# Another order of the pieces of five interleaved sequences on four engines

## What is computed

```python
def _L0_attn(x):            # block A and C of the kernel
    q, k, v = split(x @ W_qkv.T + b_qkv)               # 8 heads of 16
    qq, kq, vq = encode(q), encode(k), encode(v)        # x / |x| * exp(i * phase)
    q_ent, k_ent = entangle(qq), entangle(kq)           # 3 layers of gates between neighbouring heads
    pattern = einsum('bsid,bsjd->bsij', conj(q_ent), k_ent)   # heads against heads, in each row
    for c in range(4):                                  # 4 circuits
        probs = softmax(g[c] * abs(pattern) ** 2)
        weighted = einsum('bsij,bsjd->bsid', sqrt(probs + 1e-12), vq) * coh
        final += sup_w[c] * clipped(weighted)
    return real(final) @ W_out.T + b_out
def _L0_ffn(x):             # block B: silu(x @ wg.T) * (x @ wu.T) @ wd.T, hidden 384
def _L1_attn(x):            # block E and part of D: causal attention, 16 heads of 8, 256 rows
def _L1_ffn(x):             # part of D (routing) and the stage behind the loop: 8 experts,
                            # each takes its 64 best rows of a sequence, gelu, 512 hidden
```

## Time and profile before

| | us |
|---|---|
| median of 3 runs | 2605.27 |
| lowest and highest of them | 2596.32, 2612.04 |
| the profiled execution | 2586.84 |
| its span, first to last instruction | 2585.0 |
| DVE busy | 1998.8 (77%) |
| PE busy | 1995.3 (77%) |
| POOL busy | 1428.3 (55%) |
| ACT busy | 1283.5 (50%) |
| granted clock of PE, mean | 0.882 |

### The profile page before, as it was taken

How to read it: one execution, slowest core, us unless ns; L and a number is a source line. 1 busy time by engine, 2 the same in 40 slices (tenths; PEclk the granted TensorE clock), 3 DMA queues, 4 the chain that set the end, 5 groups by cost and what they waited for, 6 DMA issues and landing times.

```text
span 2585.0 us, 45044 instructions
## 1 busy us (share of the span) xinstructions
PE 1995.3 (77%) x15068; PEld 1548.3 (60%) x15068; DVE 1998.8 (77%) x3422; ACT 1283.5 (50%) x2989; POOL 1428.3 (55%) x1104
## 2 busy tenths in 40 slices
PE   1357877888877888787788788888788787289999
PEld 0346666666666666666666666666666664157777
DVE  4888999989989998999999999899999852502221
ACT  1125555555555555555555555555555555033332
POOL 2666666666666665666666666666666510364310
PEclk8688899889899988989988988888988887589999
DMA  3000000000000000000000000000000000112210
GB/s 89 2 7 9 9 8 8 8 8 8 8 8 8 9 9 6 8 9 9 8 8 8 8 8 8 8 8 8 8 8 6 6 5 5 34 44 63 56 45 24
DMA packets 64565, 39.38 MB, mean 15 GB/s; under 512 B 9350, under 2 KB 60431, under 8 KB 64528
## 3 DMA queue, kind: packets, MB, share of 16 engines
q1 hardware_dynamic: 54238, 26.30, 3.6%
q0 software_dynamic: 4096, 8.40, 1.2%
q10 hardware_dynamic: 6194, 4.21, 0.6%
HBM read 26.31 MB, written 12.58 MB: 15 GB/s over the span
## 4 chain that ended last, share of the span: by engine, by line
POOL 32%; PE 25%; issue 19%; DVE 17%; ACT 5%; ACTq 1%; POOLq 0%; DVEq 0%; DMA 0%
POOL arena L649 10%; POOL arena L657 8%; PE pa L1296 4%; PE pd L1286 4%; DVE arena L629 4%; PE pb L1036 4%; POOL arena L461 4%; POOL arena L662 3%; POOL arena L629 3%; POOL arena L458 2%; PE pa L732 2%; DVE arena L525 2%; PE pd L1027 2%; DVE state L529 2%; PE pd L1024 2%
## 5 line engine op out<-in xcount | busy, mean ns | idle before, releaser
L751 PE MATMUL pa<-ident,arena 128*128 128x128 f32 x4096 | 545.9, 291 | 99.9 <-POOL arena L629 66.4
L751 PEld LDWEIGHTS pa<-ident,arena 128*128 128x128 f32 x4096 | 514.8, 205 | 122.7 <-POOL arena L629 79.9
L649 POOL TENSOR_TENSOR arena<-arena,neg_half 128x32 f32<-128x32 f32 x64 | 269.4, 4226 | 281.9 <-DVE arena L495 281.9
L1036 PE MATMUL pb<-ident,arena 128*128 128x128 f32 x1536 | 304.7, 313 | 138.2 <-ACT arena L931 84.2
L657 POOL TENSOR_TENSOR arena<-state,c_cross 128x448 f32<-128x448 f32 x128 | 241.6, 1908 | 226.6 <-DVE state L518 188.2
L1036 PEld LDWEIGHTS pb<-ident,arena 128*128 128x128 f32 x1536 | 194.6, 158 | 271.4 <-issue 172.9
L931 ACT ACTIVATE arena<-pb 128x384 f32<-128x384 f32 x512 | 253.9, 496 | 155.9 <-PE pb L1036 151.3
L629 DVE TENSOR_TENSOR arena<-arena 128x1024 f32<-128x1024 f32 x192 | 311.8, 1638 | 4.1 <-PE pa L751 3.3
L924 ACT ACTIVATE arena<-pd,arena 128x256 f32<-128x256 f32 x512 | 245.7, 480 | 0.0
L458 POOL TENSOR_TENSOR arena<-arena,eps_t 128x2 f32<-128x2 f32 x128 | 126.8, 991 | 213.4 <-DVE arena L490 125.8
L923 ACT ACTIVATE arena<-pd,arena 128x128 f32<-128x128 f32 x512 | 189.6, 370 | 37.7 <-DVE arena L811 36.6
(11 more groups left out here) (246 smaller groups left out, 4577.0 us busy)
## 6 DMA issues: line engine op xcount, KB each, us to landing
x_land<-in_L_attn_query SPq DMA_DIRECT2D x32, 128.0 KB, 2.1
arena<-in_L_attn_query SPq DMA_DIRECT2D x32, 128.0 KB, 2.1
x_scratch<-x SPq DMA_DIRECT2D x32, 128.0 KB, 1.8
xn_scratch<-xn_d SPq DMA_DIRECT2D x32, 128.0 KB, 1.8
arena<-x_scratch SPq DMA_DIRECT2D x16, 256.0 KB, 3.0
out_x<-arena SPq DMA_DIRECT2D x16, 256.0 KB, 2.4
w<-in_L_ffn_W ACTq DMA_DIRECT2D x1, 2048.0 KB
arena<-xn_scratch,arena POOLq DMA_INDIRECT x128, 2.5
```

What stands on the lines that cost most here:

```text
L649: g.tensor_tensor(of_tile(rnorm)[:, :, c], of_tile(ssq)[:, :, c], of_tile(neg_half)[:, :, c], ALU.pow).then_inc(S("a_rnorm"), 1)
L751: mm = pe.matmul(pa[:, t, c * P:c * P + P], wprod[:, k % NWP, j * 128:j * 128 + 128], ident[:, :], start=(j == 0), stop=(j == NH - 1))
L1036: mm = pe.transpose(pb[:, j * P:j * P + P], p_raw[:, s % 3, j * P:j * P + P], ident[:, :])
```

## The change

Only the four order strings change. The pieces, their number and the waits in them stay as they are.

```diff
-POOL_ORDER = "A1C2B1A3C1A1B1A2C1D1C1D1"
-ACT_ORDER = "E7A1E3A1E4B1E2A1E5B1E1C1E1B1E2C1E3A1E2B1E3C1E4A1E3C1A1D1B1D1C1D2"
-PE_ORDER = "E5A1E3A1E4B1E3B1E7B1E2B1E3C1E1C1E1C1E1C1D1C1D1C1D1C2D2C2"
-DVE_ORDER = "C1A1C1A1C1B1C1E1C1E1B1C1E1C2E1C1A1C1A1C1E1C4B1C1B1E1C2A1E1B1C1B1C1A1E1A1B1C1A1C2B1A1B1C1A2C1A1D2C1A1C1D3C1A2C2D2A1D1A1D1C1"
+POOL_ORDER = "A1C2B1A4C1B1A2C1D1C1D1"
+ACT_ORDER = "E7A1E1A1E3A1E5B1E4B1E3C1A1E2B1E3C1E3B1A1E2C1E6A1E1B1D1C1D1C1D2"
+PE_ORDER = "E4A1E1A1E6B1E4B1E7B1E2B1E3C1E1C1E1C1E1C1D1C1D1C1D1C2D2C2"
+DVE_ORDER = "C1A1C1A1C1B1C1E1B1E1C2A1E1C1A1C1E1C2E1C2A1C1E1A1C1B1C1B1A1C1E1A1C2B1C1B1C1E1B1A1C1A1C2B2A2C2A1D2C2D3C1A2C2D2A1D2A1C1"
```

## The result

The changed kernel takes 2469.24 us (median of 4, 2466.69 to 2473.79) against 2606.97 for the kernel before; the ratio is 0.948, interval 0.945 to 0.951. The profiled span fell from 2585.0 to 2464.9, by 120.1.

A forecast was written before the change was run, and what follows sets the result against it. Bound: DVE and POOL taking turns on two-operand SBUF work, the lap ended by a chain beginning on POOL. 28 laps x (64.2 - 61.9) = 64 us; 2586.8 - 64 = 2523, median 18.4 above: 2541, range 2512 to 2605.

The forecast's parts named there:

- the layout: New lap laid out by hand from old durations, each wait at its latest releaser: lap 61.9 us, 64.2 before.
- PE at offsets 5 to 17: Early qkv at 1.2 GHz: L494 and E3 each wait 0.9 us; DVE 0.2 behind at E4, bounds 0 to 2.
- rival 3: Slower: PE at 1.2 GHz past offset 15.9 delays scores of pairs 3 and 4, and k=0, by 1.4 us; chance 0.13.
- turns at 1.2 GHz past offset 16: Sign on PE that would show the prediction wrong.
- The unrolled laps: Laps outside the loop: same pieces with less to collide, nothing taken for them, bounds -6 and +6 us.
- Powers: POOL's L649 pair runs from 15.2 to 23.6 and does not block DVE; nothing charged.
- rival 2: No gain: waits at E3 and blocking return it; lap 64.2, chance 0.12. Strict form: powers hold L564 2.2 us, lap 64.1.
- Blocking: Two-operand work of DVE and POOL never runs together; losses 5.9 us a lap before, 3.6 blocked in the new lap.
- The tie: DVE's third L629 gets the shared port pair ahead of POOL's L629 (k=3), by about 0.05 us.
- Rival 1: POOL takes the pair first for k=3, at 38.55; L637 blocked 1.9 us; lap 63.3, 2580 us; chance 0.20.
- The price of later probabilities: DVE's L585 ends at 33.0, so k=0 begins at 35.2 instead of 33.8; POOL's k=3 must wait until 38.5.
- The end of the lap: Old chain of 7.9 us after k=7 at 53.2, plus 0.6 for L612's wait: 61.7; 61.9 taken.

The follow-up runs named there:

- x9: Changed kernel with PE's work ahead of the scores of pair 2 made some 3 us longer by repeated matmuls: 2603.89 us, ratio 0.964, lap 61.4.
- x2: Kernel before with PE's new order and only ACT's early moves (A2, A3), DVE and POOL as before: ratio 1.008, lap 64.8.
- x4: Kernel before with 24 more matmuls a lap that nobody reads, at PE's idle places: ratio 1.003, lap 64.8.
- x3: Changed kernel with PE's old order, ACT's A2, A3 and DVE's A3, A4 at their old places (no early qkv): ratio 1.016, lap 65.4.
- x7: x3 with POOL's two powers L649 made plain products of constants: median 2563.15 us, ratio 0.948, lap 60.5.
- x6: Changed kernel with POOL's old order (k=3 ahead of L662): ratio 0.989, lap 63.7.

## Why the forecast was right in kind and half as large as the gain

*Offsets of the layout beside the lap shown above and the mean of the 28 laps* (us after L553):

| step | forecast | lap shown | mean |
|---|---|---|---|
| L494 begins | 11.0 | 10.9 | 10.6 |
| scores of pair 2 read (E3) | 12.9 | 11.8 | 11.5 |
| first L649 | 15.2 | 14.1 | 13.8 |
| L505 | 22.4 | 21.3 | 21.5 |
| L662 ends | 33.9 | 32.7 | 32.9 |
| L585 ends | 33.0 | 31.7 | 31.9 |
| k=0 begins | 35.2 | 33.9 | 34.1 |
| k=3 ends | 41.5 | 40.2 | 40.5 |
| L529 of layer 1 ends | 43.5 | 42.3 | 42.6 |
| k=7 ends | 53.2 | 51.8 | 52.0 |
| lap ends | 61.9 | 60.0 | 60.5 |

- **The step that failed: PE at offsets 5 to 17.** From E3 to k=7 the layout is off by one constant against the lap shown, 1.1 to 1.4 us (0.9 to 1.4 against the mean), and it arises at E3. I carried over the stretch at 1.2 GHz of the kernel before (ten us at a granted clock of 0.51), and had turn 1 and the scores of pair 2 run at that speed. In the changed kernel the same place of this lap has 0.76 over seven us:

```profile
1093.00:1100.00 7.00, 5.63 (x25) 3.31 (x25) 6.21 (x7) 5.51 (x15) 5.09 (x6) 0.76 0.06 19
```

  Slow in it are the turn just ahead of qkv (three L1036 from 1093.53, 0.90 us; 0.49 behind qkv) and qkv itself. The scores behind it are not:

```profile
1094.22 2.66 PE L732 MATMUL pa<-w_qkv_t,xnt_a 128*128 128x384 f32 x4
...
1097.68 0.60 PE L1027 MATMUL pd<-arena 32*128 32x256 f32 x4
```

  The wait there was to cost 1.8 us a lap (L494 and E3). L494 and L810 together cost 26.3 us over 28 laps, 0.9. The bound I had set, 0 to 2 us behind at E4, had zero as its lower end, and no term for being ahead. x9, which lengthens just this stretch, shows that such a shift reaches k=7 whole. The other laps agree: the scores of pair 2 end between 10.0 and 11.6 in all 28, never at 12.9, and in 9 of them qkv too runs at full clock (7.1 to 8.6). The row of the kernel before was a fair one, as its clock is low there in all its 28 laps (from between 5.5 and 8.1 to between 13.2 and 16.6). The mistake was to carry it into another order. x2 (order) and x4 (added matmuls) show that it moves with what PE is given.
- **A low stretch that I did not lay out, where rival 3 had it.** In 9 of the 28 laps the clock is low again from about 13.5 to 20.3, and the scores of pairs 3 and 4 come late. One such lap (L553 at 1267.60): the stretch, and DVE's wait for pair 4:

```profile
1281.00:1287.90 6.90, 6.90 (x41) 4.13 (x43) 6.29 (x7) 3.92 (x12) 6.11 (x2) 0.51 0.00 0
```

```profile
1288.73 0.42 DVE L810 TENSOR_REDUCE arena<-pd 128x2 f32<-128x256 f32 x1 [1.32 <-PE pd L1027]
```

  This is one of the signs that the prediction gave for being wrong (turns at 1.2 GHz past offset 16), and it came true in a third of the laps. These 9 take 62.2 us in the mean, the other 19 take 59.8. So the layout's 61.9 is 2.1 too long for a lap without that stretch, and close to a lap with it only by luck.
- **The unrolled laps.** I took nothing for them, with 6 us on either side, as having less to collide. The three intervals of L553 ahead of the loop went from 56.9, 58.2 and 65.3 us to 51.1, 54.0 and 61.1, 14.2 together. They have A, C and POOL's products like the others; blocks E and D, and with them the chain at the lap's end, stand only in the third. Counted like laps of the loop they would have carried 4 us each, which is what the second and third gained (4.2).
- **Sum of the miss.** 120 - 64 = 56 us: 28 laps x 1.35 = 38 (61.9 to 60.55), 14 ahead of the loop, 1 behind it, and 3 from the lap of before (64.2 in the sum, 64.3 in the mean). The other 16 of the 72 us are not the kernel's: I put the median 18.4 us above the profiled execution, as before, and it came out 2.6 above (2469.24 and 2466.69).
- **Powers.** Right: L649 ran from 1100.96 to 1109.24, over L564 and L505, and these took 0.42 and 0.69, no more than elsewhere. The strict form of rival 2 is refuted. x3 and x7 show that the powers matter only through their end.
- **Blocking.** Right: 4.4 us a lap forecast (L557 0.57, L585 0.3, then 1.25, 1.0, 0.3, 1.0), 3.6 measured. Each was in its place, none off by more than some 0.4 in the mean. The first L657 pair had 2.35 for a forecast near 2.
- **The tie.** DVE's third L629 went first, as laid out: its pair stands at 2.35, and POOL's L629 at 2.96, which is 1.1 of waiting and 1.9 of its own. Rival 1 did not happen in any of the 28 laps.
- **The price of later probabilities.** Sized too high with all else by the constant; k=0 begins at 33.9, as in the kernel before (33.8), and the product k=3 ends 2 us earlier in the lap (42.6 before, 40.2). In the means k=0 begins 0.8 later (33.2 before, 34.1) and k=3 ends 1.7 earlier (42.2, 40.5).
- **The end of the lap.** 8.7 forecast behind k=7 (61.9 - 53.2), 8.5 measured in the mean.
- **Rival 3** had the clock as its mechanism too. For pairs 3 and 4 it was right in the 9 laps above; over the whole loop the clock went the other way (0.90 to 0.93).

No single part carries the gain: POOL's order alone costs 0.6%, early qkv alone 0.8%, all without early qkv 1.6%, and together they save 5.2%. All but POOL's swap saves 1.1% (x6). DVE's new order by itself was not run. What stays open is how much of the 1.35 us a lap is the clock at E3. The offsets of the lap shown say all of it, x9 says that up to half of such a shift comes back at the end, the 9 laps with a second low stretch lose again what the others win, and x7 reaches the same lap with low clock and 1.6 us of waits for scores. Nor is it shown why the clock is low in some laps at 13.5 to 20.3 and not in others.

## What to carry to other kernels

Sums and products of DVE and POOL with both operands in SBUF behaved here as one queue (the powers did not): write both engines' orders side by side and put POOL's large operations beside DVE's reductions, PSUM operands and waits. Such an order is worth something only when the producer of its early pieces (here the powers, behind qkv) comes early as well, so test the orders of all engines together, and do not drop one that loses alone. In a layout by hand take a stretch of low PE clock as a range that includes its absence and another place, look at all laps and not at one, and count unrolled laps like the rest.

## What the hardware showed beyond that

POOL's tiny operations are held up by DVE as well: L458 (2 elements a partition) took 1.04 us at 1127.02, beside DVE's L527, and 0.19 at 1138.56. During the 8.3 us of powers none of DVE's operations was longer than elsewhere. Matmuls put into PE's idle places did raise the mean clock in x4 (0.90 to 0.93), but low stretches came back elsewhere in the lap (L789, L849), and the time stayed.
